# Four features selected once per chunk for six product tiles, in grouped operations

## The reference

```python
e = jnp.stack([tbl_0[ids[:, 0]], ..., tbl_38[ids[:, 38]]], axis=1)      # 512 x 39 x 16
def _cin(X0, weights):                                                    # W0: 39*39 x 128, W1: 39*128 x 128
    Xi, res = X0, []
    for W in weights:
        z = jnp.einsum('bmd,bnd->bdmn', X0, Xi)
        Xi = jnp.einsum('bdp,po->bod', z.reshape(b, d, 39 * mi), W)
        res.append(Xi)
    return jnp.sum(jnp.concatenate(res, axis=1), axis=-1)                 # 512 x 256
h = jnp.concatenate([_cin(e, [W0, W1]), dense_ctx], axis=1)               # 512 x 272
h = jnp.maximum(h @ W_top1 + b_top1, 0.0)
h = jnp.maximum(h @ W_top2 + b_top2, 0.0)
y = h @ W_top3
```

## Time and profile before

| | us |
|---|---|
| median of three runs | 263.35 |
| the profiled execution, as a run | 262.94 |
| its span | 260.9 |
| PE busy in it | 235.9 |
| DVE busy | 196.1 |
| ACT busy | 168.6 |
| POOL busy | 128.8 |

### The profile page before, as it was taken

How to read it: one execution, slowest core, us unless ns; L and a number is a source line. 1 busy time by engine, 2 the same in 40 slices (tenths; PEclk the granted TensorE clock), 3 DMA queues, 4 the chain that set the end, 5 groups by cost and what they waited for, 6 DMA issues and landing times.

```text
span 260.9 us, 5243 instructions
## 1 busy us (share of the span) xinstructions
PE 235.9 (90%) x1848; PEld 182.4 (70%) x1848; DVE 196.1 (75%) x341; ACT 168.6 (65%) x324; POOL 128.8 (49%) x180
## 2 busy tenths in 40 slices
PE   4998856989799978939999999999999999999996
PEld 4997733555466754737777777777787888898795
DVE  1799969998879999556889999879989877624001
ACT  4997555675787886547759878686757655466203
POOL 4788888888888888878888882000000000000000
PEclk9999755899999999988999999999999999999999
DMA  5920001545026540200221111010110101010000
GB/s 160 233 45 10 9 5 13 112 83 129 8 27 147 122 96 7 28 8 9 45 33 20 24 11 28 5 25 7 21 16 12 25 1 25 4 25 0 3 0 0
DMA packets 30883, 10.30 MB, mean 39 GB/s; under 512 B 21018, under 2 KB 30138, under 8 KB 30858
## 3 DMA queue, kind: packets, MB, share of 16 engines
q1 hardware_dynamic: 27722, 9.17, 16.3%
q0 software_dynamic: 3136, 0.81, 3.5%
HBM read 7.34 MB, written 0.00 MB: 28 GB/s over the span
## 4 chain that ended last, share of the span: by engine, by line
PE 48%; POOL 26%; DVE 12%; issue 9%; ACT 3%; DMA 2%; DVEq 0%; ACTq 0%
POOL feat L355 21%; PE s_bank L964 11%; POOL pad L353 5%; PE b_bank L904 4%; PE l_bank L925 4%; PE l_bank L927 4%; PE l_bank L926 4%; DVE z L716 3%; DVE w_sb L660 3%; DVE z_lo L730 3%; PE g_bank L949 2%; PE g_bank L950 2%; PE g_bank L951 2%; PE xi_bank L934 1%; ACT g L448 1%
## 5 line engine op out<-in xcount | busy, mean ns | idle before, releaser
L355 POOL DMA_INDIRECT feat<-tbl,ids_sb x98 | 107.3, 1095 | 29.4 <-POOL pad L353 21.1
L716 DVE TENSOR_TENSOR z<-xa,b_bank 128x512 f32<-128x512 f32 (+1 forms) x112 | 76.1, 684 | 17.3 <-PE b_bank L904 13.8
L529 ACT ACTIVATE z_hi<-z 128x512 fp32r<-128x512 f32 (+1 forms) x104 | 65.6, 630 | 18.9 <-DVE z L716 17.5
L730 DVE TENSOR_TENSOR z_lo<-z,z_hi 128x512 fp32r<-128x512 f32 x88 | 60.3, 686 | 0.0
L904 PE MATMUL b_bank<-xs,sel 117*128 117x512 bf16 (+1 forms) x112 | 45.2, 406 | 8.7 <-DVE z L716 8.6
L964 PE MATMUL s_bank<-g,w_sb 128*128 128x128 f32 x312 | 46.3, 278 | 0.0
L964 PEld LDWEIGHTS s_bank<-g,w_sb 128*128 128x128 f32 x312 | 42.2, 192 | 1.3 <-issue 0.7
L925 PE MATMUL l_bank<-z_hi,w_hi 128*128 128x512 f32 x88 | 41.8, 474 | 0.0
L904 PEld LDWEIGHTS b_bank<-xs,sel 117*128 117x128 bf16 (+1 forms) x112 | 11.5, 103 | 38.3 <-DVE z L716 20.7
L537 ACT ACTIVATE g<-g_bank 128x320 f32<-128x320 f32 x64 | 27.7, 432 | 16.3 <-PE g_bank L951 16.0
L927 PE MATMUL l_bank<-z_hi,w_lo 128*128 128x512 f32 x88 | 35.1, 399 | 0.0
(11 more groups left out here) (190 smaller groups left out, 368.2 us busy)
## 6 DMA issues: line engine op xcount, KB each, us to landing
diag<-xt SPq DMA_DIRECT2D x128, 20.0 KB
w_sb<-w SPq DMA_DIRECT2D x3, 832.0 KB
feat<-tbl,ids_sb POOLq DMA_INDIRECT x98, 2.4
wt_sb<-wt SPq DMA_DIRECT2D x2, 512.0 KB, 4.7
g<-small SPq DMA_DIRECT2D x1, 770.0 KB
g<-small SPq DMA_DIRECT2D x1, 448.0 KB
w0p<-w_pair SPq DMA_DIRECT2D x1, 448.0 KB
w0m<-w_mirror SPq DMA_DIRECT2D x1, 448.0 KB
```

Source lines behind the costliest of these rows:

```text
L355: nc.gpsimd.indirect_dma_start(feat[:, bt % 2, n * D:(n + 1) * D], None, tables[order[n]], bass.IndirectOffsetOnAxis(ids_sb[:, bt, order[n ...
L529: nc.scalar.activation(z_hi[0:rows, s % RING, :], z[0:rows, at, :], ACT.Copy).then_inc(rounded, 1)
L716: nc.vector.tensor_tensor(target, xa[0:rows, bt % 2, c * CB:(c + 1) * CB, :].rearrange("p b d -> p (b d)"), b_bank[s % B_RING][0:rows, :], ...
L730: nc.vector.tensor_sub(low[first:rows, s % RING, :], z[first:rows, SPLITS[s] % Z_RING, :], z_hi[first:rows, s % RING, :].bitcast(f32)).the ...
```

## The change

**Four factors, six products.** The 780 products are laid out anew. Each partition now holds four features, and the six products of two of them fill tiles 0 to 5. So four selections per chunk do instead of eight: the first factor (fill_a) and three more, and ACT copies two of these from PSUM to SBUF (take_factor, new), beside the first, into `factors`. The fourth stays in its bank, and so does a selection for the products that are left over (the rest tile, number 6, three times as before); selections of q = 0 to 3 come at the steps of SELECT_AT, counted from the chunk's first, and for the first chunk of tiles 2 and 3 at TILE_SELECT_AT.

**Groups.** The seven tiles of a chunk are made in four groups, of 2, 1 (the rest), 3 and 1 tiles, at steps 0, 2, 3 and 6 of the chunk (GROUPS: first step, count, slot, place in z). Product, rounding and subtraction of a group are one instruction each, of up to 1536 columns. The subtractions stand at steps 2, 4, 6 and 8. The products of groups 0 and 3 read SBUF alone, the other two also a bank. Layer 1 takes the tiles in the order 0, 1, rest, 2, 3, 4, 5 (T_OF).

**No direct step.** All chunks are split in all tiles (DIRECT_CHUNKS = 0).

**Later splits.** For tiles 2 and 3 the last split of gathered rows moves from step 19 (21) to step 23 of the tile before, the transposes from 21 (23) to 25, the first fill_a from 24 (26) to 27.

**Also:** the splitting of W0 stands ahead of the copy of the first chunk's features on DVE; the weights of the rest tile are made by two instructions with a mask instead of three copies; a third factor of chunk 0 is copied by DVE.

```diff
 PARTS = 3
 R = PARTS * F
 PAIRS = F * (F + 1) // 2
-PT = -(-PAIRS // P)
-REST = PAIRS - (PT - 1) * P
-REST_AT = (0, F, 2 * F)
-REST_LO = 64
-REST_ROWS = 96
-ROWS = [P] * (PT - 1) + [REST_ROWS]
-assert REST <= F and REST_AT[1] >= 32 and REST_AT[1] + REST <= REST_LO <= REST_AT[2] and REST_AT[2] + REST <= REST_ROWS
+PT = 7
+FACTORS = 4
+PRODUCTS = ((0, 1), (0, 2), (3, 0), (3, 1), (3, 2), (1, 2))
+REST_T = PT - 1
+REST_LO = slice(64, 98)
+T_OF = (0, 1, REST_T, 2, 3, 4, 5)
+GROUPS = ((0, 2, 0, 0), (2, 1, REST_T, 2), (3, 3, 2, 3), (6, 1, 5, 2))
+GROUP_AT = {first: k for k, (first, count, slot, at) in enumerate(GROUPS)}
+REST_AT_STEP = {2: 0, 4: 1, 6: 2, 8: 3}
+GROUP_OF = [next(k for k, g in enumerate(GROUPS) if g[0] <= u < g[0] + g[1]) for u in range(PT)]
+NG = len(GROUPS)
+SELECTS = 4
...
-DIRECT = [[1, 4], [], [], []]
+DIRECT_CHUNKS = 0
 WHOLE = 2
-Z_LAG = 2
-Z_RING = Z_LAG + 2
-LEAD = 1
+Z_SLOTS = 6
 RING = LAG + 2
+assert RING == PT
...
-SPLIT_AT = [[], [8, 14, 19], [8, 14, 19], [9, 16, 21]]
-X_AT = [[], [21, 22], [21, 22], [23, 24]]
-A_AT = [0, 24, 24, 26]
+SPLIT_AT = [[], [8, 14, 19], [9, 16, 23], [9, 16, 23]]
+X_AT = [[], [21, 22], [25, 26], [25, 26]]
+A_AT = [0, 24, 27, 27]
+SELECT_AT = [-4, -2, -1, 0]
+TILE_SELECT_AT = [None, [-4, -2, -1, 0], [0, 0, 1, 2], [0, 0, 1, 2]]
...
+def select_step(i, q):
+
+    bt, c = divmod(i, CPT)
+    return i * PT + (TILE_SELECT_AT[bt] if bt and c == 0 else SELECT_AT)[q]
+
+
+SELECT_STEPS = {}
+for i in range(CHUNKS):
+    for q in range(SELECTS):
+        SELECT_STEPS.setdefault(select_step(i, q), []).append((i, q))
...
+                if i >= 2:
+                    act.wait_ge(product, NG * (i - 1))
+                nc.scalar.activation(factors[:, i % 2, 0, :], turn_banks[k][:], ACT.Copy).then_inc(turn_taken[k], 1)
+
+            def take_factor(i, k):
+
+                act.wait_ge(selected, SELECTS * i + k + 1)
+                if i >= 2:
+                    act.wait_ge(product, NG * (i - 1))
+                nc.scalar.activation(factors[:, i % 2, 1 + k, :], b_bank[k][:], ACT.Copy).then_inc(factor_taken, 1)
...
-            def round_z(s):
-                rows = ROWS[s % PT]
-                if direct(s):
+            def round_z(i, k):
+                if direct(i, k):
                     return
-                at = SPLITS[s] % Z_RING
-                act.wait_ge(product, s + 1)
-                if s >= RING:
-                    act.wait_ge(l1_used, s - RING + 1)
-                nc.scalar.activation(z_hi[0:rows, s % RING, :], z[0:rows, at, :], ACT.Copy).then_inc(rounded, 1)
+                first, count, slot, at = GROUPS[k]
+                act.wait_ge(product, NG * i + k + 1)
+                if i:
+                    act.wait_ge(l1_used, (i - 1) * PT + first + count)
+                nc.scalar.activation(z_hi[:, slot:slot + count, :], z[:, at:at + count, :],
+                                     ACT.Copy).then_inc(rounded, 1)
...
-                if s < STEPS:
-                    round_z(s)
+                for i, q in SELECT_STEPS.get(s, []):
+                    if q < 2 and i:
+                        take_factor(i, q)
+                if s < STEPS and s % PT in GROUP_AT:
+                    round_z(s // PT, GROUP_AT[s % PT])
...
-            def multiply(s):
-                i, t = divmod(s, PT)
-                bt, c = divmod(i, CPT)
-                rows = ROWS[t]
-                if direct(s):
-                    number = s - SPLITS[s]
-                    if number == 0:
-                        dve.wait_ge(zeroed, 4)
-                    if number >= WHOLE:
-                        dve.wait_ge(l1_used, DIRECT_STEPS[number - WHOLE] + 1)
-                    target = whole[number % WHOLE][0:rows, :]
+            dve.wait_ge(selected, 2)
+            nc.vector.tensor_copy(factors[:, 0, 2, :], b_bank[1][:]).then_inc(third_taken, 1)
...
+            def multiply(i, k):
+
+                if k == 0:
+                    for q in range(2):
+                        dve.wait_ge(*taken_factor(i, q))
+                    dve.wait_ge(*after(turn_taken, "a", i, 0))
+                    z_free(i - 1, 0)
+                    target = z[:, 0:2, :]
+                    one = factors[:, i % 2, 0, :].unsqueeze(1).broadcast_to([P, 2, CH])
+                    other = factors[:, i % 2, 1:3, :]
+                elif k == 1:
+                    dve.wait_ge(selected, SELECTS * i + 3)
+                    z_free(i - 1, 1)
+                    z_free(i - 1, 3)
+                    target, one, other = z[:, 2, :], factors[:, i % 2, 0, :], b_bank[0][:]
+                elif k == 2:
+                    dve.wait_ge(selected, SELECTS * i + 4)
+                    z_free(i - 1, 2)
+                    target = z[:, 3:6, :]
+                    one = factors[:, i % 2, :, :]
+                    other = b_bank[1][:].unsqueeze(1).broadcast_to([P, 3, CH])
                 else:
-                    if SPLITS[s] >= Z_RING:
-                        dve.wait_ge(remainder, SPLITS[s] - Z_RING + 1)
-                        dve.wait_ge(rounded, SPLITS[s] - Z_RING + 1)
-                    target = z[0:rows, SPLITS[s] % Z_RING, :]
-                if t == 0:
-                    dve.wait_ge(*after(turn_taken, "a", i, 0))
-                dve.wait_ge(selected, s + 1)
-                nc.vector.tensor_tensor(target,
-                                        xa[0:rows, bt % 2, c * CB:(c + 1) * CB, :].rearrange("p b d -> p (b d)"),
-                                        b_bank[s % B_RING][0:rows, :], ALU.mult).then_inc(product, 1)
-
-            def rest_z(s):
-                if direct(s):
+                    if direct(i, k):
+                        if i == 0:
+                            dve.wait_ge(zeroed, 4)
+                        if i >= WHOLE:
+                            dve.wait_ge(l1_used, (i - WHOLE + 1) * PT)
+                        target = whole[i % WHOLE][:]
+                    else:
+                        z_free(i, 1)
+                        target = z[:, 2, :]
+                    one, other = factors[:, i % 2, 1, :], factors[:, i % 2, 2, :]
+                nc.vector.tensor_tensor(target, one, other, ALU.mult).then_inc(product, 1)
+
+            def rest_z(i, k):
+                if direct(i, k):
                     return
-                rows = ROWS[s % PT]
-                dve.wait_ge(rounded, SPLITS[s] + 1)
-                if s >= RING:
-                    dve.wait_ge(l1_used, s - RING + 1)
-
-                low = z_lo if s % PT < PT - 1 else z_hi
-                first = 0 if s % PT < PT - 1 else REST_LO
-                nc.vector.tensor_sub(low[first:rows, s % RING, :], z[first:rows, SPLITS[s] % Z_RING, :],
-                                     z_hi[first:rows, s % RING, :].bitcast(f32)).then_inc(remainder, 1)
+                first, count, slot, at = GROUPS[k]
+                dve.wait_ge(rounded, SPLITS[i, k] + 1)
+                if i:
+                    dve.wait_ge(l1_used, (i - 1) * PT + first + count)
+                if k == 1:
+                    nc.vector.tensor_sub(z_hi[REST_LO, slot, :], z[REST_LO, at, :],
+                                         z_hi[REST_LO, slot, :].bitcast(f32)).then_inc(remainder, 1)
+                else:
+                    nc.vector.tensor_sub(z_lo[:, slot:slot + count, :], z[:, at:at + count, :],
+                                         z_hi[:, slot:slot + count, :].bitcast(f32)).then_inc(remainder, 1)
 
...
-                if Z_LAG <= s < STEPS + Z_LAG:
-                    rest_z(s - Z_LAG)
+                for at, k in REST_AT_STEP.items():
+                    if (i := chunk_at(s, at)) is not None:
+                        rest_z(i, k)
...
-            def select(s):
-
-                i, t = divmod(s, PT)
-                bt, c = divmod(i, CPT)
-                if s >= B_RING:
-                    pe.wait_ge(product, s - B_RING + 1)
-                if t == 0:
+            def select(i, q):
+
+                if q == 0:
                     features_there(i)
-                nc.tensor.matmul(b_bank[s % B_RING][0:ROWS[t], :], sel[:, t, 0:ROWS[t]], columns(bt, c),
+                if q < 2:
+                    if i:
+                        pe.wait_ge(product, NG * (i - 1) + 2 + q)
+                else:
+                    pe.wait_ge(*taken_factor(i, q - 2))
+                nc.tensor.matmul(b_bank[q % B_RING][:], sel[:, q, :], columns(*divmod(i, CPT)),
                                  start=True, stop=True).then_inc(selected, 1)
...
+                elif t == REST_T:
+                    nc.tensor.matmul(bank[:], w0_rest[:], z_hi[:, t, :], start=False, stop=False).then_inc(l1_used, 1)
                 else:
-                    nc.tensor.matmul(bank[:], w0_hi[:, t, :], z_hi[:, slot, :], start=t == 0, stop=False)
-                    nc.tensor.matmul(bank[:], w0_hi[:, t, :], z_lo[:, slot, :], start=False, stop=False)
-                    nc.tensor.matmul(bank[:], w0_lo[:, t, :], z_hi[:, slot, :],
```

(5 more changed lines are left out.)

221 lines of the change are left out of this document (137 added, 84 removed).

## The result

The changed kernel takes 273.58 us (median of six runs, 272.89 to 275.07) against 263.35 in the same comparison: ratio 1.0385, 95% interval 1.0351 to 1.0419. It is slower, as forecast, but by 10.2 us instead of 2.2, and outside the range. The profiled execution, the longest of the six, took 275.07 us as a run, with a span of 273.0.

What follows compares the result with a forecast made beforehand. Bounds in turn: VectorE in tiles 0 and 1, gathers at tile 2's start, then TensorE. After the change tile 3's gathers decide: 167.8 + 3.9 + 4.8 + 86.8 = 263.3 us span; forecast 265.5, range 262.5 to 268.5, with other cases 258 to 270.

Steps and rivals of the forecast that it cites:

- 247.0 + the holding: End of the span if tile 3's gathers decide: 263.3 us with 16.3 of holding; 13.9 would mean no change.
- The gate of tile 3 decides: At tile 3's start, TensorE would be ready at 169.5 us, but the gathers allow its transposes only at 171.7.
- wrong if the last gather starts before 160: Stated test of the forecast: the last gather should start near 165 us rather than 157.4.
- The rule for one gather: A gather starting inside a VectorE operation with two SBUF inputs is held until 0.13 us before its end.
- they may fall into step: Caveat that held gathers may align with VectorE's row, so holding could be less; low end 0.11 us a gather.
- The first rival: Gathers held no more than now (8.4 us), TensorE unbroken after tile 2's gate: 259.8 us as a run; chance 0.30.
- VectorE's arrival at tile 2's gate: VectorE reaches tile 2's gathered rows at 115.6 us instead of 108.1: +3.4, -1.0 and +5.1.
- held gathers and coarse groups add up: Rival: 0.30 us holding a gather, 0.5 more per chunk in tiles 0 and 1; 271 as a run; chance 0.13.
- From a landing to TensorE: At the gates of tiles 2 and 3, landing to transposes takes 3.9 us instead of 2.0, 1.9 more each.
- TensorE's g block: TensorE waits for take_g behind the three-tile rounding: 0.55 us a chunk, 1.3 once at starts of tiles 2 and 3.
- Three selections fewer: TensorE does three selections fewer per chunk at 0.23 us each: -0.7 of 11.24 us.
- Late splits: Tile 2's last split four steps later: VectorE arrives 5.1 us later, winning those steps whole if gathers landed at 113.5.

Runs made afterwards that it cites:

- g_first_quiet: The changed kernel with take_g ahead of round_z in each step of ScalarE's loop, on an even chip: 265.67 us, 1.0048 of the kernel before.
- early_quiet: The changed kernel with splits, transposes and first selections of tiles 2 and 3 at tile 1's steps, on an even chip: 270.64 us, 1.026.
- round_single: The changed kernel with the three-tile rounding as three instructions, each waiting for its own slot only: 268.76 us, 1.0198 of the kernel before.
- no_pause: The changed kernel without the memset and the wait for it ahead of each gather of tiles 1 to 3: 270.93 us, 1.024.

## Why the prediction was wrong

- **Direction** right by luck, size wrong: 265.5 forecast, 273.6 measured, outside 258 to 270. The forecast was slower only because the gathers were to be held for more than 13.9 us. With the 10.1 that were measured its own formula, 247.0 + the holding, gives 257.1, faster than before; the measured span is 15.9 us above that. The span was to be 263.3 and is 273.0. Of the 9.7 us, 7.8 lie ahead of tile 3's transposes (171.7 forecast, 179.51) and 1.9 behind (91.6 forecast, 93.5).
- **"The gate of tile 3 decides"**, the step that failed. The forecast held the gathers for 16.3 us; they were held for 10.1. The last starts at 159.6, and under "wrong if the last gather starts before 160" I had named it. The gate did not decide at all: VectorE waits for rows at neither tile 2 nor tile 3, and those of tile 3 lie there some 12 us before it comes. What stood in its place is the ring of ScalarE and TensorE: the three-tile rounding waits 17.2 us for layer 1 and the g blocks 14.8 us for the copies behind it, and with the copies first the change falls to 1.0048, though its last gather then starts at 162.9, later still. The rule for one gather holds in the kernel after, the mean did not: I let gathers fall anywhere in VectorE's row. The rule applied to the 74 gathers with the real starts of VectorE's instructions gives 10.35 us of 10.45; spread evenly over the same row they would be held 17.6, so the missing part is that they do not fall evenly; the caveat "they may fall into step" was the case. Why they do is not shown. In the kernel before the same rule gives only 5.6 of 8.5 us: five gathers (86.42, 97.14, 99.54, 114.14 and 150.55), four of them begun under the rest tile's 96-partition product with a bank and one under a memset, were held 2.8 us that it does not cover. So the mean of before agreed with the reckoning in part for another cause, which is open. The first rival (gathers no more held than now) had this right and yet the wrong sign, 259.8, for it took TensorE's row as unbroken. The Trainium skill ("SBUF — State Buffer", section "Who interferes with whom") infers that tensor_tensor does not hold up descriptor generation; the 2.42 us under the subtraction of 83.37 contradict that here too.
- **VectorE's arrival at tile 2's gate**: 115.6 forecast, 122.20 measured. I summed VectorE's work, and its work was about right (forecast about 1 us less over the whole, measured 195.9 against 196.1). I left out that the coarse groups put it in a ring with the other two engines: 3.47 us at 83.37 for a rounding that waits for TensorE, and the way into tile 1 at a low clock. The rival "held gathers and coarse groups add up", 271 at 0.13, was the nearest in size, but not in cause: it needed 0.30 us of holding a gather, where 0.14 was measured, and its handshakes lay between VectorE and ScalarE, not between ScalarE and TensorE.
- **From a landing to TensorE**: 3.9 forecast, 4.9 measured at tile 2 (122.20 to 127.06). The 1.0 is the rounding's wait for its slot, which I had priced for take_g and not for keep_next behind the same instruction.
- **TensorE's g block**: 0.55 a chunk and 1.3 at the starts of tiles 2 and 3 forecast; about right in tile 3 (0.45, 0.61 and 0.59 us at 195.69, 207.08 and 231.89; chunks 11.1 forecast, 11.39 and 11.18 measured), far too small over the whole: 14.8 us in 17 waits, before 3.2 in 5, and 10.7 of the 14.8 lie ahead of tile 3's transposes. The place, the cause and the instruction were as written; the sum counted only the chunks behind tile 3's gate, since I thought that everything ahead of it was covered by the gathers. g_first_quiet shows that it was not: 8.9 us of the 10.2 go with it.
- **Three selections fewer** is right: TensorE has 6.8 us less to do.
- **Late splits**: I took 1.9 us at each gate as the price and the 5.4 us wait as the stake. The stake was won (no wait for rows), and VectorE then waits 7.41 and 6.68 us for the late factors, which the forecast did not count; against early_quiet the change pays 4.3 us between chunks 6 and 8 and 2.6 between 8 and 11, and gains only 4.0 between 5 and 6.
- Left open: why gathers and VectorE's subtractions fall into step; what held the five gathers in the kernel before; what the low clock alone costs on the way into tile 1; and how much of g_first's 8.9 us belongs to the ring itself and how much to instructions behind it. No run separates these.

## What to carry to other kernels

When instructions are grouped, ask of the grouped one what it waits for last, and what stands behind it on its engine: a group waits for the latest of its slots, and a copy that another engine needs at once must stand ahead of it. Count such a wait in every chunk, also where something else seems to be the bound, for the bound may move. A right sign with a wrong mechanism is no success: put the measured value of each term back into the sum and see whether the sign stays. And test the parts of a change apart: here one part gained 1.2% alone, the other lost 2.6%, and together they lost 3.85%.

## What the runs showed of the hardware

- TensorE's clock fell into its lower level (1.2 of 2.4 GHz) at tile 1's start after idle pieces of 1.45 (to 67.33), 1.45 (to 71.78) and 2.07 us (to 75.19), granted 0.62 from 72 to 78 us, and stayed at 1.00 over the same stretch with 1.63 (to 68.00) and 1.91 us (to 74.20) in round_single. Eight transposes took 1.11 against 0.63 us. Such pieces alone do not tell a fall from none: no_pause has 1.45 us too (to 66.21), and its clock was granted 0.72 from 66 to 72, where the change had 1.00.
- A gather that starts inside a VectorE product or subtraction with both inputs in SBUF is held until 0.13 us before that instruction's end, for 1536 columns as for 512: 10.35 us by this rule against 10.45 seen over 74 gathers of the kernel after. In the kernel before the rule gives 5.6 of 8.5 us, and what held five more gathers is not known.
- A 1536-column product or subtraction takes 1745 to 1762 ns on VectorE, so the estimate of 0.54 us per 512 columns held; its rounding on ScalarE takes 1485.
